# Local attention of a four-layer network: the rotary product taken from a second matmul with exchanged halves, written in place, and a new order of the attention rounds

## The reference, cut to what matters

```python
h = shift_token(x)                       # upper 64 channels one token later
q, k, v = split(h @ wqkv)                # 8 heads of 64
q = l2norm(q) * q_scale;  k = l2norm(k) * k_scale
# rotate_half(t) = concat(-t[32:64], t[0:32]) within a head
q = q * cos * scale + rotate_half(q) * sin * scale
k = k * cos / scale + rotate_half(k) * sin / scale
o = local_attention(q, k, v)             # windows of 64, each with the one before
x = x + o @ wo
x = x + gated_gelu_ffn(layernorm(shift_token(x)))
```

## Time and profile before

| what | value |
|---|---|
| median of 3 runs | 4255.21 us (4247.0 to 4261.16) |
| the profiled execution, its own time | 4256.1 us |
| its span | 4253.9 us |
| mean granted TensorE clock | 0.919 |
| busy TensorE, its weight loads, VectorE, ScalarE, GpSimd | 3659.6, 2097.3, 2656.3, 2155.1, 861.8 us |
| the eight local blocks start at | 2935.07, 3054.99, 3293.68, 3415.93, 3648.80, 3768.79, 4003.75, 4124.30 us |
| transfers into lkt and lqt | 256 and 256, 64.0 KB each, some 2.0 us to land |

### The profile page before, as it was taken

One profiled execution on the slowest core, in us unless ns is written; L12 is line 12 of the kernel. 1 busy time (PEld: TensorE's weight loads), 2 busy tenths in 40 slices (PEclk: granted clock), 3 DMA queues, 4 the chain that ended last, 5 costly groups with the idle time before them and its releaser, 6 DMA issues. The chain is left out here.

```text
span 4253.9 us, 74287 instructions
## 1 busy us (share of the span) xinstructions
PE 3659.6 (86%) x27416; PEld 2097.3 (49%) x27416; DVE 2656.3 (62%) x5977; ACT 2155.1 (51%) x4957; POOL 861.8 (20%) x1067
## 2 busy tenths in 40 slices
PE   5988878888989996899899899988878887887887
PEld 3655654444545543333333333445555665555555
DVE  5667646565555654776766767736655665665665
ACT  3555554554555453565555655754554554444454
POOL 1111000000010002122232132124212331431421
PEclk8999988988999898899999999989998998999999
DMA  3222301111101102111011111002120230321112
GB/s 107 62 48 45 77 20 47 36 24 31 36 17 43 29 13 91 28 32 38 17 43 32 23 37 33 15 38 62 37 71 23 61 80 8 79 61 27 53 42 54
DMA packets 146011, 183.15 MB, mean 43 GB/s; under 512 B 29972, under 2 KB 99796, under 8 KB 142324
## 3 DMA queue, kind: packets, MB, share of 16 engines
q1 hardware_dynamic: 139748, 170.93, 16.0%
q10 hardware_dynamic: 5904, 7.48, 0.7%
HBM read 91.69 MB, written 34.08 MB: 30 GB/s over the span
## 5 line engine op out<-in xcount | busy, mean ns | idle before, releaser
L1266 ACT ACTIVATE prob<-ps_st 128x512 f32<-128x512 f32 (+3 forms) x2432 | 1120.6, 511 | 1127.9 <-PE ps_st L1208 586.4
L1299 DVE TENSOR_REDUCE mhalf<-mx 128x1 f32<-128x512 f32 (+3 forms) x2064 | 1265.7, 652 | 658.4 <-PE mx L1240 324.4
L1237 PE MATMUL mx<-ks,qs 72*128 72x512 bf16 (+3 forms) x2304 | 793.2, 373 | 130.2 <-DVE g_tok L1874 52.5
L1205 PE MATMUL ps_st<-qs,ks 75*128 75x512 bf16 (+3 forms) x2432 | 780.5, 355 | 66.3 <-ACT prob L1266 44.5
L1188 PE MATMUL ps_o<-prob,vst 128*32 128x512 f32 (+3 forms) x5376 | 580.0, 514 | 0.1
L1237 PEld LDWEIGHTS mx<-ks,qs 72*128 72x128 bf16 x2304 | 232.4, 103 | 558.3 <-DVE mhalf L1299 192.7
L1205 PEld LDWEIGHTS ps_st<-qs,ks 75*128 75x128 bf16 x2432 | 243.1, 101 | 327.7 <-ACT prob L1266 172.1
L1349 POOL COPY vst<-v_tok 128x256 f32<-128x256 f32 x48 | 19.9, 418 | 1218.4 <-PE ps_o L1188 1217.2
L3202 ACT ACTIVATE o<-ps,nm,lrq 128x128 f32<-128x128 f32 x512 | 227.0, 462 | 43.9 <-DVE nm L3317 43.7
L1188 PEld LDWEIGHTS ps_o<-prob,vst 128*32 128x32 f32 x5376 | 114.5, 111 | 178.9 <-ACT prob L1266 78.8
L2278 POOL TENSOR_SCALAR ffn_small<-bcs,table 80x128 f32<-80x128 f32 x256 | 148.9, 603 | 122.9 <-PE mx L2406 115.6
(11 more groups left out here) (476 smaller groups left out, 6394.2 us busy)
## 6 DMA issues: line engine op xcount, KB each, us to landing
qs<-q_scr SPq DMA_DIRECT2D x279, 96.0 KB
ks<-k_scr SPq DMA_DIRECT2D x135, 192.0 KB
lkt<-o SPq DMA_DIRECT2D x256, 64.0 KB, 2.0
lve<-lv SPq DMA_DIRECT2D x24, 512.0 KB, 4.5
lqt<-o SPq DMA_DIRECT2D x160, 64.0 KB, 2.0
tabs<-local_tables SPq DMA_DIRECT2D x4, 2048.0 KB, 8.0
k_scr<-part SPq DMA_DIRECT2D x30, 256.0 KB, 3.1
lqt<-o ACTq DMA_DIRECT2D x96, 64.0 KB, 2.1
```

The lines of the kernel that those rows point to most:

```text
L1205: last = nc.tensor.matmul(ps_st[:, u % 3, 0:q1 - q0], ks[g % 2][0:KR, h, kt * P:(kt + 1) * P], qs[g % 2][0:KR, hf, h, q0 - hf * HALF:q1 - ...
L1237: last = nc.tensor.matmul(bank[:, j * w:(j + 1) * w], qs[g % 2][0:R, hf, h0 + j, (t - 4 * hf) * P:(t - 4 * hf + 1) * P], ks[g % 2][0:R, h0 ...
L1266: nc.scalar.activation(prob[:, b % PROBS, h, 0:q1 - q0], ps_st[:, u % 3, 0:q1 - q0], ACT.Exp, scale=scale).then_inc(S["exped"], 1)
L1299: nc.vector.tensor_reduce(mhalf[:, hf, h0:h0 + heads, t - 4 * hf, part], bank[:, 0:heads * (k1 - k0)].rearrange("p (n w) -> p n w", n=head ...
```

## The change

- The weights keep their order of columns. A unit of work is now a head pair: u = 2n + j, two to a step. Its first product (bank 0) is the pair's 128 channels. Its second product (bank 1) gives the same channels with the 32-channel halves of each head exchanged, as four products of 32 columns of weights, each into its own strip of 32 output partitions.
- The sine table has its sign in it, so GpSimd only adds. VectorE writes the cosine product right into `lqt` or `lkt`, GpSimd adds the sine product there, `k_units` multiplies there. The placing transfers, the semaphores `placed` and `both` and the addition of squares are gone.
- `sums` has eight products of two columns in place of four products of four columns; `spread` has two groups of eight products into strips of 64 in place of sixteen into strips of 32, and counts `k_spread` twice.
- The PSUM buffers go by pair and not by step. Fillers: three ahead of every value product but the first (before: five in each step from the third on), and six ahead of the first round. The values' product uses one bank.
- The rounds have the order turn(2t), weigh(2t-1), turn(2t+1), scores(t+2), turn_out(t-1), weigh(2t), project(t-2); VectorE's order becomes maxima(2t+2), residual(t-3), copies(2t), normalise(t-1), maxima(2t+3), copies(2t+1). `pr`, `ptr`, `och` and `gg` get memory of their own or other memory.
- SP issues the two value shifts first thing; each depth has its own pair of semaphores for them.

```diff
+    v = np.asarray(v)
+    return np.tile(np.stack([v, np.roll(v, 32)], 1), (2, 1))
...
-    parts.append(("ones32", (np.arange(P)[:, None] // 32 == np.arange(P)[None, :] // 32) * 1.0))
+    parts.append(("ones64", (np.arange(P)[:, None] // 64 == np.arange(2)[None, :]) * 1.0))
...
+    signed = lambda a: np.tile(np.concatenate([-a.T, a.T], 0), (2, 1))
...
+            def tile_of(n, j):
+                m, g, i = pairs[n]
+                return (qt, kt)[m][:, 2 * g + j, i * HALF:(i + 1) * HALF]
...
-            pr, ptr = (o[:, k, :, :].rearrange("p s (i c) -> p s i c", i=4) for k in range(2))
+            pr = net.g_tok[:, :, :].rearrange("p (g i) c -> p g i c", g=2)
+            ptr = net.tmp("ptr", [P, 2, 4, P])
...
-                    for k in range(0, NT, 2):
-                        if k == NT - 2:
-                            shift_values(sp, 1)
-                        for n, s in ((k + 1, 0), (k, 0), (k, 1)) if k < NT - 2 else ((k + 1, 0), (k + 1, 1), (k, 0), (k, 1)):
-                            finished(sp, n, s)
-                            for b in range(4):
-                                place(sp, n, s, b)
-                        if k == 2:
-                            shift_values(sp, 0)
-                    for k in range(4):
-                        sp.wait_ge(placed[k], 128 * 2)
+                    for i in range(2):
+                        shift_values(sp, i)
...
-                        pe.wait_ge(S["both"], n + 1)
+                        pe.wait_ge(S["sq"], 2 * n + 2)
...
-                            last = nc.tensor.matmul(pss[:, c0:c0 + 4], sq[n % 2][:, 0, t * P:(t + 1) * P], net.K("ones32")[:, 0:P:32],
-                                                    start=True, stop=True)
+                            for j in range(2):
+                                last = nc.tensor.matmul(pss[:, c0 + j:c0 + 4:2], sq[n % 2][:, j, t * P:(t + 1) * P], net.K("ones64"),
+                                                        start=True, stop=True)
...
+                            for j in range(2):
+                                for t in range(4):
+                                    for e in range(2):
+                                        c0 = 4 * t + 2 * e + j
+                                        last = nc.tensor.matmul(prk[j][D * e:D * e + D, t * P:(t + 1) * P],
+                                                                rk[:, n // 2 % 2, c0:c0 + 1].broadcast_to([P, D]), net.ident, start=True, stop=True)
+                                last.then_inc(S["k_spread"], 1)
...
-                        if n >= 2:
-                            pe.wait_ge(S["v"], n - 1)
-                            keep_clock(net, pv[:, n % 2, :], 5)
-                            pe.wait_ge(S["prod"], 4 * (n - 1))
-                            pe.wait_ge(S["sq"], 2 * (n - 1))
-                        for s in range(2):
-                            c0 = m * IN + (2 * g + s) * P
-                            last = nc.tensor.matmul(pab[:, n % 2, s, :], W(f"l3_wqkv{d}")[:, c0:c0 + P], ch[:, i * HALF:(i + 1) * HALF],
-                                                    start=True, stop=True)
-                        last.then_inc(S["qkmm"], 1)
...
+                        for j in range(2):
+                            u = 2 * n + j
+                            if u >= 2:
+                                pe.wait_ge(S["prod"], 2 * (u - 1))
+                                pe.wait_ge(S["sq"], u - 1)
+                            c0 = m * IN + (2 * g + j) * P
+                            w, y = W(f"l3_wqkv{d}"), ch[:, i * HALF:(i + 1) * HALF]
+                            nc.tensor.matmul(pab[:, u % 2, 0, :], w[:, c0:c0 + P], y, start=True, stop=True)
+                            for b in range(4):
+                                c = c0 + 32 * (b + 1 - 2 * (b % 2))
+                                last = nc.tensor.matmul(pab[32 * b:32 * b + 32, u % 2, 1, :], w[:, c:c + 32], y, start=True, stop=True)
+                            last.then_inc(S["qkmm"], 1)
...
+                        if n >= 1:
+                            pe.wait_ge(S["v"], n)
+                            keep_clock(net, pv[:, 0, :], 3)
...
                         if t in (0, 4):
-                            for p in placed:
-                                pe.wait_ge(p, 128 if t == 0 else 256)
+                            pe.wait_ge(S["rot"], NT if t == 0 else 2 * NT)
+                            pe.wait_ge(S["k_unit"], 4 if t == 0 else NT)
...
+                    pe.wait_ge(S["v"], NT)
+                    keep_clock(net, pv[:, 0, :], 6)
                     for t in range(NT):
                         turn(2 * t)
+                        if t >= 1:
+                            weigh(2 * t - 1)
                         turn(2 * t + 1)
                         if t + 2 < NT:
                             scores(t + 2)
-                        weigh(2 * t)
                         if t >= 1:
                             turn_out(t - 1)
-                        weigh(2 * t + 1)
+                        weigh(2 * t)
                         if t >= 2:
                             project(t - 2)
+                    weigh(2 * NT - 1)
...
                         if u == 0:
-                            act.wait_ge(placed[0], 256)
+                            act.wait_ge(S["rot"], 2 * NT - 2)
...
+                            nc.vector.scalar_tensor_tensor(out=x[n % 2][:, j, :], in0=pab[:, j, 1, :], scalar=scale[m][:, 1:2], in1=sin,
+                                                           op0=ALU.mult, op1=ALU.mult).then_inc(S["prod"], 1)
+                            dve.wait_ge(S["sq"], u + 1)
+                            nc.vector.scalar_tensor_tensor(out=tile_of(n, j), in0=pab[:, j, 0, :], scalar=scale[m][:, 0:1], in1=cos,
+                                                           op0=ALU.mult, op1=ALU.mult).then_inc(S["prod"], 1)
...
-                        pool.wait_ge(S["sq"], 2 * n + 2)
-                        nc.gpsimd.tensor_tensor(sq[n % 2][:, 0, :], sq[n % 2][:, 0, :], sq[n % 2][:, 1, :], ALU.add).then_inc(S["both"], 1)
...
+                        for j in range(2):
+                            pool.wait_ge(S["prod"], 4 * n + 2 * j + 2)
+                            nc.gpsimd.tensor_tensor(tile_of(n, j), tile_of(n, j), x[n % 2][:, j, :], ALU.add).then_inc(S["rot"], 1)
```

More of the change, by code:

```diff
@@ L2852, in local_block @@
         v_e = kept("lve", [P, NT, IN])
-        shifted = [net.early["v_low"], net.early["v_high"]]
+        shifted = [net.early[f"v_low{d}"], net.early[f"v_high{d}"]]
         qt = kept("lqt", [P, H // 2, T])
@@ L2871, in local_block @@
             po = net.psum("po", [P, 2, IN])
-            pab, pv, pss, prk = ps[:, :, :, :, :].rearrange("p a s i c -> p a s (i c)"), pt, po[:, 0, :], po[:, 1, :]
+            pab, pv, pss, prk = ps[:, :, :, :, :].rearrange("p a s i c -> p a s (i c)"), pt, po[:, 0, :], [po[:, 1, :], pt[:, 1, :]]
             ch = net.xn_ch
             low, high = slice(0, C // 2), slice(C // 2, C)
-            placed = [S[f"placed{k}"] for k in range(4)]
             scale = [W(f"l3_qs{d}"), W(f"l3_ks{d}")]
             ksum = NT * H
[L2879 to L2885, removed]
+            def tile_of(n, j):
                 m, g, i = pairs[n]
-                e, j = divmod(b, 2)
-                queue.dma_start((qt, kt)[m][D * e + 32 * s:D * e + 32 * s + 32, 2 * g + j, i * HALF:(i + 1) * HALF],
-                                o[32 * b:32 * b + 32, n % 4, s, :]).then_inc(placed[n % 4], 16)
+                return (qt, kt)[m][:, 2 * g + j, i * HALF:(i + 1) * HALF]
             def shift_values(sp, i):
@@ L3167, in _ @@
                     for n in range(NT):
-                        act.wait_ge(S["qkmm"], n + 1)
-                        if n >= 2:
-                            act.wait_ge(S["sums"], n - 1)
-                        for s in range(2):
-                            nc.scalar.activation(sq[n % 2][:, s, :], pab[:, n % 2, s, :], ACT.Square).then_inc(S["sq"], 1)
+                        for j in range(2):
+                            act.wait_ge(S["qkmm"], 2 * n + j + 1)
+                            if n >= 2 and j == 0:
+                                act.wait_ge(S["sums"], n - 1)
+                            nc.scalar.activation(sq[n % 2][:, j, :], pab[:, j, 0, :], ACT.Square).then_inc(S["sq"], 1)
                         if n >= 1:
@@ L3175, in _ @@
                         act.wait_ge(S["vmm"], n + 1)
-                        nc.scalar.activation(v_l[:, n, :], pv[:, n % 2, :], ACT.Copy).then_inc(S["v"], 1)
-                        if n >= 2 and pairs[n - 2][0] == 0:
-                            finished(act, n - 2, 1)
-                            for b in range(4):
-                                place(act, n - 2, 1, b)
+                        nc.scalar.activation(v_l[:, n, :], pv[:, 0, :], ACT.Copy).then_inc(S["v"], 1)
                     norms(NT - 1)
@@ L3241, in k_units @@
                         if pairs[n][0] == 1:
```

(8 more changed lines are left out.)

74 lines of the change are left out of this document (23 added, 51 removed).

## The result

The changed kernel took 4412.24 us (median of 4 runs, 4411.48 to 4425.33) where the kernel before took 4251.1 beside it (4 runs, 4239.41 to 4261.16). The ratio is 1.0387, 95% interval 1.0353 to 1.0422. The forecast was 4400 us, range 4340 to 4435.

What follows compares the result with a forecast made beforehand. The prediction took TensorE's in-order queue to bound the projection stage. Stage +26.0, softmax start -3.5 and rounds -4.5 gave +18.0 us a call, +144 over eight calls on 4256.1: 4400 us, range 4340 to 4435.

Steps and rivals of the forecast that it cites:

- Part 1, the pair: Projection stage: full product plus four 32-column products cost 2.07 us a pair, 33.1 a call instead of 13.8.
- hidden whole: Projection stage: lower bound for a pair's second product, which then costs nothing; the upper bound was 3.44 us.
- mode changes cost nothing: Rival, projection stage: a pair is 1.74 us, 5.3 less a call, total 4358 us; chance 0.15.
- Part 2, sums: Projection stage: 16 instructions in place of 8, still 0.107 us each, 1.72; 12.0 a call instead of 6.0.
- Part 3, spread: Projection stage: 64-column strips two side by side, 1.87 us each spread; 5.6 in the stage instead of 3.1.
- 32-column strips one after the other: Rival, second product of a pair: strips run serially, 36 us more a call, total 4685; chance 0.04.
- Part 4, fillers: Projection stage: fillers take 4.5 us instead of 6.4, values 6.9 as before; stage after 62.1, +26.0 a call.
- Part 5, other engines: VectorE, GpSimd, ScalarE and SP: their changed work costs nothing once TensorE needs 62 us in the stage.
- Faster: Rival, projection stage: TensorE hides the second product, stage stays 36.1 us, total 4192; chance 0.03.
- Part 6, start of the softmax: Table load 3.75 us after E, the projection stage's end, instead of 7.25: -3.5 a call.
- Part 7, the rounds: Softmax rounds: 5.35 us instead of 5.77, clock 1.00; table load to last normalise 42.6 instead of 47.1, -4.5 a call.
- the new order gains nothing: Rival, rounds: a round stays 5.77 us as the moved weigh waits for its copy; 2.5 more a call, 4420; chance 0.10.

Runs made afterwards that it cites:

- no_second: Changed kernel with the four-strip second product left out, the sine product reading the first product's bank: 4280.75 us.
- full_second: Changed kernel with one full 128-column product in place of the four 32-column strips of each pair: 4377.79 us.
- grouped_strips: Changed kernel with both full products of a step first, then both groups of strips, so tiling changes twice a step, not four times: 4381.92 us.
- half_sums: Changed kernel with sums from the first pair's squares alone, four products of four columns in place of eight of two: 4355.68 us.
- more_vector: Changed kernel with one more table product for each pair on VectorE, into memory that nobody reads: 4418.78 us.
- no_gap_fillers: Changed kernel without the six fillers ahead of the first round: 4418.88 us.
- before_new_order: Kernel before, placing transfers kept, with the new order of the rounds and twenty fillers ahead of them: 4237.32 us, ratio to before 0.9975.
- before_early_softmax: before_new_order with buffers moved so the first exponentials wait for the rotation, not a transfer, and eight fillers for twenty: 4237.78 us, ratio to before 0.9978.
- before_pool_places: before_early_softmax with the last eight placing transfers of the queries issued by GpSimd instead of SP: 4208.32 us, ratio to before 0.9893.

## Why the prediction held, and where it did not

The forecast was +18.0 a call and the marks say +19.75. Over eight calls that is 14 us, against the 12 from 4400 to the 4412 measured. The stage (+25.97) and the start of the softmax (-3.58) came out within 0.1 of the sum; the miss is the rounds, with 1.86 a call.

- **Part 1, the pair: held.** 2.07 forecast from L1188, 2.05 measured. The bound "hidden whole" is ruled out by no_second, the rival *mode changes cost nothing* by full_second and grouped_strips: it set the excess at 0.33 a pair, the runs show 0.30. The model in the Trainium skill's "TensorE: Matmul & The Clock Gate", section "Measured speedup vs the span model", would have the pair at 1.74. It is close for strips among strips (0.93 a group in the mean of two, and 0.85 by difference for the second), and short by the two changes in each pair.
- **Part 2, sums: held.** Sixteen instructions took 1.70 to 1.77 against 1.72, and half_sums shows that the price hangs on instructions and not on columns, though not that the weight load is what sets it.
- **Part 3, spread: held.** 1.90 against 1.87; 64-column strips run two side by side, so that rival falls. *32-column strips one after the other* falls with the pair.
- **Part 4, fillers: held.** 0.66 against 0.64 a step. The stage came out at 62.06 against 62.1.
- **Part 5, other engines: held.** more_vector gave VectorE 10 us more work in this stage at no cost. *Faster* would have needed a stage longer by less than 8.0; it is longer by 26.0.
- **Part 6, start of the softmax: held.** E + 3.75 to the table load, as forecast; the first `turn` at E + 8.12 (2993.59 - 2985.47) against E + 8.0. The six fillers ahead of it, costed with the rest of TensorE's work there, decide nothing (no_gap_fillers).
- **Part 7, the rounds: the mechanism held, the size did not.** This is the mis-sized term: -4.5 forecast, -2.64 measured. A steady round is 5.39 to 5.40 against 5.35. But the sum ran TensorE's work through to the last `normalise` with waits only in round 2 and at the very end: 38.3 from the first `turn`, where it took 40.1 (3033.70 - 2993.59). The last rounds of the changed kernel:

```profile
3018.33 0.60 PE L3064 MATMUL pt<-table,g_tok 128*128 128x128 f32 x4
...
3023.72 0.60 PE L3064 MATMUL pt<-table,g_tok 128*128 128x128 f32 x4
...
3025.94 0.66 PE L3095 MATMUL pt<-table,in_ch 128*128 128x128 f32 x4 [0.42 <-DVE in_ch L3319]
...
3027.43 1.13 PE L3105 MATMUL pt<-stream,och 128*128 128x128 f32 x8 [0.22 <-DVE ptr L3308]
3028.40 0.60 PE L3064 MATMUL pt<-table,g_tok 128*128 128x128 f32 x4
...
3030.62 0.66 PE L3095 MATMUL pt<-table,in_ch 128*128 128x128 f32 x4 [0.41 <-DVE in_ch L3319]
```

 A round that still has scores fills the time in which VectorE normalises (3018.33 to 3023.72, 5.39, no wait). From round 6 on there are no scores, so `turn_out` waits for `normalise` and `project` for a copy: 0.42, 0.22 and 0.41, 1.05 in all. The other 0.8 is in small pieces, the largest 0.35 in round 1, which took 4.69 (2996.93 to 3001.62) for work of 4.34. That the missing scores let these waits through is read from this trace; no run puts other work in their place. The rival *the new order gains nothing* was half right for this reason: the rounds do become shorter, but the order brings 0.62 a call and not the 2.5 by which that rival was priced. That difference is the whole miss: the other 2.0 of the 4.5 came (2.02).
- **Part 8, the tail: held.** From the last `normalise` of call 1 to the memset of call 2 it is 29.0 in every kernel of the table.

## What to carry to other kernels

A stage that one in-order engine fills without a gap has no cover: price what is added there as a plain sum, from the nearest row of the same shape, and count the changes between full and narrow products. The products that replaced the transfers had no room here, and what was late was one issue queue. A softmax that starts without waiting for it, together with half of the queue's last sixteen issues on an idle engine, gained 1.1% with the new order of the rounds; removing all of it by products lost 3.9%. When a loop is reordered, price its first and last turns by themselves, because the work that fills the steady turn is missing there.

## What was not expected of the hardware

- A change from full products to four 32-column strips and back costs 0.29 us (grouped_strips, from eight saved a call), while two groups of four strips in a row cost 1.85, little over the 1.72 of two full products.
- Fillers did not hold the clock reliably. In before_new_order it fell to 0.50 in all eight calls (from 2966 on in call 1), behind twenty fillers and, in call 1, waits of 0.70 and 1.04; in no_gap_fillers it stayed at 1.00 in all eight, with no fillers and, in call 1, waits of 0.18 and 1.14. The waits are longer in sum where it fell, but no run changes that alone, so what tells the two apart stays open.
- SP's issues of the last placing transfers took 0.63 to 1.12 us each (5.01 and 8.15 for eight in before_early_softmax, 8.94 in before_pool_places), GpSimd's 0.52 (4.14 for eight). The eight right behind the two value shifts are the slow ones in both kernels; why is not shown.
- The stretch between two rows of the batch, which no kernel here changes, took 141 to 142 or 145 to 147 us, now one and now the other. The start of call 1, also behind unchanged code, moved by up to 32 us from trace to trace. Together they are most of the scatter of the totals.
